# Turning the normalised rows of eight of sixteen query chunks by DMA instead of TensorE

## The reference

```
kv = x @ W.T;  K, V = split(kv);  a = softmax(x @ K.T + causal) @ V
x1 = layernorm(x + (x + a))
xr, xk = mu * x1 + (1 - mu) * x1 of the token before
y  = layernorm(x1 + x1 + sigmoid(xr @ W_r.T) * (relu(xk @ W_k.T)**2 @ W_v.T))
```

## Time and profile before

| | us |
|---|---|
| three runs | 1156.16, 1182.71, 1183.41 |
| median of them | 1182.71 |
| the profiled execution, its own time | 1158.02 |
| its slowest core (core 5), first to last instruction | 1156.5 |
| its other cores | 1151.0 to 1155.3 |
| outside the span: 1158.02 less 1156.5 | 1.5 |

### The profile page before, as it was taken

How to read it: one execution, slowest core, us unless ns; L and a number is a source line. 1 busy time by engine, 2 the same in 40 slices (tenths; PEclk the granted TensorE clock), 3 DMA queues, 4 the chain that set the end, 5 groups by cost and what they waited for, 6 DMA issues and landing times.

```text
span 1156.5 us, 18353 instructions; the slowest of 8 cores (1151.0 to 1156.5 us)
## 1 busy us (share of the span) xinstructions
PE 1142.9 (99%) x6138; PEld 599.4 (52%) x6138; DVE 609.2 (53%) x907; ACT 448.1 (39%) x737; POOL 275.7 (24%) x354
## 2 busy tenths in 40 slices
PE   8999999999999999999999999999999999999996
PEld 3444444444444455454454557888874444444442
DVE  3545555633343142454432457876666675576865
ACT  4443333432232021223211334666564443336664
POOL 0000000000000011122111234533223333279882
PEclk9999999999999999999999999999999999999999
DMA  7455366653153152456546665776436654566662
GB/s 190 138 178 166 108 200 200 200 173 101 49 160 119 28 95 75 119 170 163 146 116 169 174 187 147 226 213 198 144 122 188 192 167 135 174 227 231 224 219 91
DMA packets 141932, 182.77 MB, mean 158 GB/s; under 512 B 44048, under 2 KB 95504, under 8 KB 141840
## 3 DMA queue, kind: packets, MB, share of 16 engines
q1 hardware_dynamic: 134512, 155.92, 45.0%
q0 software_dynamic: 7328, 25.69, 7.6%
HBM read 108.18 MB, written 64.49 MB: 149 GB/s over the span
## 4 chain that ended last, share of the span: by engine, by line
PE 98%; DVE 1%; DMA 1%; issue 0%; ACT 0%; DVEq 0%; POOLq 0%; ACTq 0%
PE ps L736 27%; PE ps L737 27%; PE ps L738 27%; PE ps L905 3%; PE ps L904 3%; PE ps L903 3%; PE ps L906 3%; PE ps L907 3%; PE ps L902 3%; PE ps L825 1%; DMA STG<-x 1%; PE ps L750 0%; PE ps L755 0%; PE ps L754 0%; DVE X L1194 0%
## 5 line engine op out<-in xcount | busy, mean ns | idle before, releaser
L669 POOL TENSOR_TENSOR SU<-TP 128x256 f32<-128x256 f32 x48 | 42.4, 883 | 184.3 <-DVE TP L1084 136.0
L1143 DVE TENSOR_TENSOR OUT<-SN,ps 128x512 f32<-128x512 f32 x94 | 63.9, 680 | 35.6 <-PE ps L738 34.6
L637 POOL DMA_DIRECT2D Z<-xtok x16 | 8.8, 553 | 289.2 <-PE ps L738 288.3
L1143 DVE TENSOR_TENSOR SN<-SN,ps 128x512 f32<-128x512 f32 x72 | 49.2, 683 | 37.9 <-PE ps L738 37.0
L706 POOL DMA_DIRECT2D x1t<-XTS x32 | 24.4, 764 | 173.2 <-ACT XTS L1349 173.2
L1333 ACT ACTIVATE PROB<-ps,NEGM 128x512 f32<-128x512 f32 (+3 forms) x36 | 22.6, 633 | 104.0 <-DVE NEGM L1036 104.0
L1349 ACT COPY XTS<-ps 128x512 f32<-128x512 f32 x32 | 18.4, 585 | 112.6 <-PE ps L825 112.6
L1068 DVE SCALAR_TENSOR_TENSOR Z<-ps,RZ,Z 128x512 f32<-128x512 f32 x16 | 12.0, 749 | 73.8 <-PE ps L907 72.9
L1455 ACT ACTIVATE OUT<-OUT 128x512 f32<-128x512 f32 x32 | 20.1, 627 | 65.0 <-DVE OUT L1143 64.9
L684 POOL TENSOR_TENSOR X<-X,RR 128x512 f32<-128x512 f32 x30 | 40.8, 1372 | 11.2 <-DVE RR L1185 11.1
L670 POOL TENSOR_TENSOR SU<-TP 128x256 f32<-128x256 f32 x48 | 41.4, 862 | 6.9
(11 more groups left out here) (449 smaller groups left out, 3504.6 us busy)
## 6 DMA issues: line engine op xcount, KB each, us to landing
STG<-x1t SPq DMA_DIRECT2D x64, 256.5 KB, 4.2
STG<-x SPq DMA_DIRECT2D x56, 256.0 KB, 4.8
WA<-wc SPq DMA_DIRECT2D x28, 512.0 KB, 6.0
Z<-xtok POOLq DMA_DIRECT2D x16, 512.0 KB, 4.5
x<-Z POOLq DMA_DIRECT2D x16, 512.0 KB, 4.2
x1t<-XTS POOLq DMA_DIRECT2D x32, 256.0 KB, 2.8
ka<-OUT SPq DMA_DIRECT2D x32, 256.0 KB, 3.4
r<-OUT SPq DMA_DIRECT2D x32, 256.0 KB, 2.6
```

The costliest lines, as they stand in the source:

```text
L669: step(gp.tensor_tensor(s1, a21, a22, op=ALU.add))
L1143: ve.tensor_tensor(out, a, ps, op=ALU.add).then_inc(count, 1)
```

## The change

Chunks at `POS` 0 to 7 (15, 3, 14, 2, 13, 1, 0, 12; `BY_DMA = 8`) are no longer transposed by TensorE. A float32 is seen as two 16-bit words. POOL copies the high words and then the low words of each half row of `Z` into a buffer `ZP[i]`, two copies of 128 x 512 words for each half, four per chunk. SP turns each `ZP[i]` with one DMA transpose into `ZT[i]`. ACT puts the words together again in `XTS[i]`, two copies with a step of two words for each half. POOL stores `XTS` as before.

The steps are spread over turns: POOL's copies of a chunk come in the turn after its own, SP's transposes (`turn_rows`) stand in the second turn after its own, behind that turn's probabilities, ACT's copies stand in the third, ahead of the exponentials, and POOL's store of chunk m - 2 stands behind its copies of chunk m. The other eight chunks keep the way through TensorE, and all of their `flip_x` stand at the end of a turn. The loads of `XQ[1]` (`xq1a`, `xq1b`), their casts, and the loads of weight slots 6 and 4 move one turn on. The new buffers take 8 KB per partition; for them the memory that POOL's DMAs keep for descriptors is cut from 16,384 to 8,192 bytes per partition.

```diff
-BASE = 16_416
+SCRATCH = 8192
+BASE = SCRATCH + 32
-    nc = bass.Bass("TRN2", target_bir_lowering=False)
+    nc = bass.Bass("TRN2", target_bir_lowering=False, dynamic_dma_scratch_size=SCRATCH)
+    ZP = [at(f"ZP{i}", [128, 1024], U16, oY + i * 2 * KB) for i in range(2)]
+    ZT = [at(f"ZT{i}", [128, 1024], U16, oY + 4 * KB + i * 2 * KB) for i in range(2)]
-    CASTS = {12: N["xq1a"], 11: N["xq1b"]}
+    CASTS = {11: N["xq1a"], 10: N["xq1b"]}
@@ SP
+        def turn_rows(q):
+            for i in range(2):
+                sy.wait_ge(g_zp, t_x(q, i) + 1)
+                if POS[q] > 0:
+                    sy.wait_ge(a_xt, t_x(q, i) - 1)
+                sy.dma_start_transpose(out=ZT[i].rearrange("p (c s) -> p c s", s=128), in_=ZP[i]).then_inc(ld_zt[i], 16)
         for q in ORDER:
             for g in range(G(q)):
                 turn(q, g)
+            if 2 <= POS[q] < BY_DMA + 2:
+                turn_rows(ORDER[POS[q] - 2])
-            elif q == 0:
+            elif q == 12:
                 loads(N["xq1a"][0], N["xq1b"][0] + 1)
-            elif q == 12:
+            elif q == 11:
                 stored(sy.wait_ge, range(12))
...
@@ POOL
+        def store_x1t(m):
+            q = ORDER[m]
+            for i in range(2):
+                gp.wait_ge(a_xt, 2 * m + i + 1)
+                dst = x1t_d[i * 512:(i + 1) * 512, (q + 1) * 128:(q + 2) * 128].rearrange("(c p) s -> p c s", p=128)
+                gp.dma_start(out=dst, in_=XTS[i].rearrange("p (c s) -> p c s", s=128)).then_inc(st_xt[i], 16)
             gp.dma_start(out=x1_d[q * 128:(q + 1) * 128, :], in_=Z[m % 2]).then_inc(st_x1[m % 2], 16)
-            for i in range(2):
-                gp.wait_ge(a_xt, 2 * m + i + 1)
...
+            if m < BY_DMA:
+                for i in range(2):
+                    if m > 0:
+                        gp.wait_ge(ld_zt[i], 16 * m)
+                    words = Z[m % 2][:, i * 512:(i + 1) * 512].bitcast(U16).rearrange("p (s w) -> p w s", w=2)
+                    gp.tensor_copy(ZP[i][:, 0:512], words[:, 1, :])
+                    gp.tensor_copy(ZP[i][:, 512:1024], words[:, 0, :]).then_inc(g_zp, 1)
+                if m > 1:
+                    store_x1t(m - 2)
+            else:
+                if m == BY_DMA:
+                    store_x1t(m - 2)
+                    store_x1t(m - 1)
+                store_x1t(m)
             if m < 14:
                 gp.wait_ge(st_x1[m % 2], 16 * (m // 2 + 1))
+                if m < BY_DMA:
+                    gp.wait_ge(g_zp, 2 * m + 2)
                 load_z(ORDER[m + 2])
@@ TensorE
-            elif q in (0, 12):
-                scores(SCORES[q][0:1])
-                flip_x(13 if q == 0 else 1, 0)
-                flip_x(13 if q == 0 else 1, 1)
-                scores(SCORES[q][1:])
...
-                if g == n - 1 and q < 15 and n > 1:
+                if g == n - 1 and POS[q] > BY_DMA:
                     flip_x(prev, 0)
@@ ACT
         def rows_t(q, i):
+            if POS[q] > 0:
                 sc.wait_ge(st_xt[i], 16 * POS[q])
+            if POS[q] < BY_DMA:
+                sc.wait_ge(ld_zt[i], 16 * (POS[q] + 1))
+                words = XTS[i].bitcast(U16).rearrange("p (s w) -> p w s", w=2)
+                sc.copy(words[:, 1, :], ZT[i][:, 0:512])
+                sc.copy(words[:, 0, :], ZT[i][:, 512:1024]).then_inc(a_xt, 1)
+            else:
+                sc.wait_ge(pe_t, t_x(q, i) - 2 * BY_DMA + 1)
+                sc.copy(XTS[i], PS[4 + i]).then_inc(a_xt, 1)
-            softmax(SCORES[q], after(q))
+            softmax(SCORES[q], after(q), ORDER[POS[q] - 3] if 3 <= POS[q] < BY_DMA + 2 else None)
```

More of the change, by code:

```diff
@@ L9 @@
 BF16 = mybir.dt.bfloat16
+U16 = mybir.dt.uint16
 AF = mybir.ActivationFunctionType
@@ L161, in build_program @@
     ld_pt = [sem(f"ld_pt{i}") for i in range(5)]
+    ld_zt = [sem(f"ld_zt{i}") for i in range(2)]
     st_o = [sem(f"st_o{i}") for i in range(3)]
@@ L338, in t_x @@
         return 2 * POS[q] + i
-    def t_bank(q, i):
-        return PS[5] if q == 15 else PS[4 + i]
+    BY_DMA = 8
     def stage(n):
@@ L702, in gpsimd_program @@
             gp.dma_start(out=x1_d[q * 128:(q + 1) * 128, :], in_=Z[m % 2]).then_inc(st_x1[m % 2], 16)
-            for i in range(2):
-                gp.wait_ge(a_xt, 2 * m + i + 1)
-                dst = x1t_d[i * 512:(i + 1) * 512, (q + 1) * 128:(q + 2) * 128].rearrange("(c p) s -> p c s", p=128)
-                gp.dma_start(out=dst, in_=XTS[i].rearrange("p (c s) -> p c s", s=128)).then_inc(st_xt[i], 16)
+            if m < BY_DMA:
[12 more added lines that the diff above has]
+                store_x1t(m)
             if m < 14:
                 gp.wait_ge(st_x1[m % 2], 16 * (m // 2 + 1))
+                if m < BY_DMA:
+                    gp.wait_ge(g_zp, 2 * m + 2)
                 load_z(ORDER[m + 2])
@@ L810, in flip_x @@
         def flip_x(q, i):
-            e = t_x(q, i)
             te.wait_ge(v_x1, POS[q] + 1)
-            if e == 0:
-                te.wait_ge(v_p, 64)
-            elif e == 1:
-                te.wait_ge(a_xt, 1)
-            elif q == 3 and i == 0:
-                te.wait_ge(a_exp, first(2) + 1)
-            elif q == 14:
+            if POS[q] == BY_DMA:
                 te.wait_ge(a_exp, first(1 - i) + 1)
             else:
-                te.wait_ge(a_xt, e - 1)
+                te.wait_ge(a_xt, t_x(q, i) - 1)
             for j in range(4):
                 c = i * 512 + j * 128
-                mm = te.transpose(t_bank(q, i)[:, j * 128:(j + 1) * 128], Z[POS[q] % 2][:, c:c + 128], IDN)
+                mm = te.transpose(PS[4 + i][:, j * 128:(j + 1) * 128], Z[POS[q] % 2][:, c:c + 128], IDN)
             mm.then_inc(pe_t, 1)
@@ L873, in tensor_program @@
                 product(0, 2, (0, 1, 2))
-            elif q == 3:
-                scores(SCORES[q][0:2])
-                flip_x(15, 0)
-                scores(SCORES[q][2:])
-            elif q == 13:
-                for i in range(2):
-                    scores(SCORES[q][i:i + 1])
-                    flip_x(14, i)
-            elif q in (0, 12):
-                scores(SCORES[q][0:1])
-                flip_x(13 if q == 0 else 1, 0)
-                flip_x(13 if q == 0 else 1, 1)
-                scores(SCORES[q][1:])
             else:
@@ L909, in tensor_program @@
                         mm.then_inc(pe_pv, 1)
-                    if g == n - 1 and j == 0 and (n > 1 or q == 3) and q < 15:
+                    if g == n - 1 and j == 0 and POS[q] > BY_DMA:
                         flip_x(prev, 1)
@@ L1345, in rows_t @@
         def rows_t(q, i):
-            sc.wait_ge(pe_t, t_x(q, i) + 1)
-            if q < 15:
+            if POS[q] > 0:
                 sc.wait_ge(st_xt[i], 16 * POS[q])
-            sc.copy(XTS[i], t_bank(q, i)).then_inc(a_xt, 1)
+            if POS[q] < BY_DMA:
[6 more added lines that the diff above has]
+                sc.copy(XTS[i], PS[4 + i]).then_inc(a_xt, 1)
         def scale(x):
@@ L1391, in high_probs, with softmax @@
                 high_p_t(q, g)
-        def softmax(blocks, nxt):
+        def softmax(blocks, nxt, turned_rows=None):
             chunks = ended(blocks)
@@ L1397, in softmax @@
                 high_probs(nxt, 0, 2)
+            if turned_rows is not None:
+                rows_t(turned_rows, 0)
+                rows_t(turned_rows, 1)
             for c in chunks:
@@ L1409, in scalar_program @@
                 high_sums(MIXES[prev])
-            if q == 3:
-                rows_t(15, 0)
-            elif q in (13, 0, 12):
-                for i in range(2):
-                    rows_t({13: 14, 0: 13, 12: 1}[q], i)
-            softmax(SCORES[q], after(q))
+            softmax(SCORES[q], after(q), ORDER[POS[q] - 3] if 3 <= POS[q] < BY_DMA + 2 else None)
             if q == 13:
@@ L1420, in scalar_program @@
                 scale(MIXES[q])
-            if G(q) > 1 and q < 15:
-                rows_t(prev, 0)
-                rows_t(prev, 1)
-            elif q == 3:
-                rows_t(15, 1)
-            if q == 12:
+            if q == 11:
                 sc.wait_ge(pe_s, first(12) + 4)
@@ L1431, in scalar_program @@
                 high_probs(after(q), at_once(after(q)), 2)
+            if POS[q] == BY_DMA + 1:
+                rows_t(ORDER[BY_DMA - 1], 0)
+                rows_t(ORDER[BY_DMA - 1], 1)
+            if POS[q] > BY_DMA:
+                rows_t(prev, 0)
+                rows_t(prev, 1)
             if q in MIXES:
```

10 lines of the change are left out of this document (4 added, 6 removed).

## The result

The changed kernel took 1177.68 us in the median of its 6 runs (1176.01 to 1293.32), the kernel before 1157.47 in the median of 6 (1156.16 to 1183.41). The ratio is 1.018, 95% interval 1.0162 to 1.0197: within 2%, but a loss of some 20 us where I had forecast a gain of 7.

The account below looks back on a forecast made before the run. TensorE was taken to bound the kernel, busy 1142.9 of 1156.5 us. From 1158.0, 64 transposes at 0.11 (7.0) were removed and no waits added, giving 1151 us; range 1147 to 1178.

Parts of the forecast that it names:

- the account itself: Whole kernel: TensorE work removed less TensorE waits added, from the profiled 1158.0 us, 7.0 less, giving 1151.0.
- something else: Any outcome outside the forecast case and the named rivals, no place or size given; chance 0.02.
- The range's top: Upper end of the predicted time, set at 1178 us from the earlier runs' 1183.41 less 7.0, which is 1176.4.
- Transposes at 0.11 each: Attention turns 1 to 8: 64 transposes leave TensorE at 0.11 us each from start to start, 7.0 us in all.
- Rival D: Each transpose removed from TensorE is worth its whole 0.273 us, 17.5 in all, time 1140.5; chance 0.03.
- The walk and the hiding: Short turns before chunk 12: its first block's transpose issued at 510.4, landing 513.8, wanted 518.1, so no TensorE wait.
- c: Time of one POOL copy of 128 x 512 16-bit words: 0.9 us taken, bounds 0.55 and 2.26.
- B: Short turns: the POOL, store, ACT, SP loop closes too slowly; TensorE waits 10.2 us, time 1161 to 1171; chance 0.1.
- A: At chunk 12, row transposes land late and TensorE waits 1.3 to 6.4 us, time 1152 to 1157.5; chance 0.2.
- The second tight place: Chunk 11's first scores wait on chunk 12's first exponential: slack 0.15 us before and after, added wait taken as 0.
- Rival C: At attention's end, a load or weight slot timed by DMA comes last and eats the gain, 1156 to 1160; chance 0.1.

Follow-up runs that it names:

- `before_again`: The kernel before, unchanged, run again: 1156.72 us at the lower level, ratio 0.9999; 1 of 9 runs at the upper level.
- `mem_only`: The kernel before with only the changed kernel's memory layout (descriptor memory 8192 bytes, buffers lower): 1156.61 us at the lower level, ratio 0.9996.
- `twice_third`: The changed kernel with each of its 64 remaining TensorE transposes issued twice, a later rerun: 1157.13 us at the lower level, ratio 1.0000.
- `no_flip`: The kernel before without TensorE's row transposes of the eight first chunks, rows left untransposed (wrong results): 1148.60 us at the lower level, ratio 0.9929.
- `twice`: The changed kernel with each of its 64 remaining TensorE transposes issued twice: 1157.70 us, ratio 0.9989, when first run; 1157.41 and 1157.13 in reruns.
- `after_fourth`: The changed kernel, unchanged, run once more: 1149.97 us at the lower level, ratio 0.9937; 3 of 6 runs at the upper level.
- `rows_early`: The changed kernel with ACT's row copies put back ahead of the casts in turns 9 to 15: 1151.91 us, ratio 0.9937; reruns 1149.04 and 1149.05.
- `no_warm`: The changed kernel with 1 instead of 10 warm-up products before the first projection: 1152.99 us, ratio 0.9953; reruns 1151.07 and 1151.02.
- `tail_pad`: `rows_early` with 64 tiny products added at the end of TensorE's list: 1150.61 us, ratio 0.9938, beside its control's 1149.05.

## Why the prediction was wrong, and where it was right

**The step that failed** is the account itself: "PE work removed less PE waits added, made against the profiled execution". It takes for granted that stages which the change doesn't touch keep their time, and it counted the 27 us between the kernel before's own runs as noise of the measurement ("three runs of one program differ by 27 us"). They are two levels of one mechanism: a granted clock of 0.81 for 161 us in the projections, on pairs of cores. The slowest core makes the time, so one pair is enough. What decides is how often it comes. Over the chips that show it at all (A, B, E), the runs of the programs with the full count of TensorE instructions (before, `before_again`, `mem_only`, `twice_third`) had it in 11 of 71 cases, those with 64 fewer and 10 warm-up products (the changed kernel, `no_flip`) in 14 of 21. By comparison it is 2 of 6 against 5 of 5 in the first, 6 of 38 against 6 of 10 on B, and 3 of 27 against 3 of 6 on E. (For the first comparison's runs of before only the times are known; two are at 1183.) So the first comparison had it in all of the changed kernel's runs and in 2 of 6 of before's, and a median turned that into plus 20 us. (The ratio of 1.018 sets runs of the changed kernel at the upper level against the four of the kernel before at the lower one, 1156 to 1158.) None of the named rivals was this; it fell under "something else", at 0.02. The range's top, 1178, was set by exactly this ("the runs of one program reach 1183.41; less 7.0 this is 1176.4") and held the time, with luck, by 0.3 us; I had priced the level rightly and its frequency not at all.

**Transposes at 0.11 each**: right. 171.81 became 164.82, and `twice` beside the changed kernel gave the 7 back (1157.41 against 1150.18, 1157.13 against 1149.97). Rival D, 0.273 each, would have been 17.5. `no_flip`, the ceiling, ends where the changed kernel ends at the lower level on chip B (two runs each).

**The walk and the hiding**: right, with errors that cancelled. One of POOL's copies takes 0.61 us, and the four in a row start 0.55 apart (496.36, then the stores at 498.58), which is the lower bound of c and not the 0.9 that I used: 1.4 us less for four. The stores' landing and ACT's copies (0.76 each and not 0.6) took 1.0 more than forecast, and SP needed 3.07 for its two issues, so that chunk 12's block came 0.75 later behind ACT than worked out. The sum is the 0.3 between 510.4 and 510.7. The row transposes landed after 3.8 in the median, 6.6 at most. B did not occur. A occurred once that I found, on core 2 of `after_fourth`: PE waits for a block of chunk 12; the four transposes of probabilities around it landed after 4.5 to 11.5 us:

```profile
524.74 0.38 PE L916 MATMUL ps<-V2H,PT 128*128 128x512 bf16 x1 [0.71 <-DMA PT<-PH]
```

It was not that core's loss that set the time. The descriptor memory cost nothing (`mem_only`).

**The second tight place**, chunk 11's first scores with 0.15 of slack: right. They start at 497.37, 0.39 behind the matmul before them, and before it was 0.38.

**Rival C**, the gain goes elsewhere, happened in part, 0 to 2.3 us per core, but not by a load or weight slot: by ACT's list, an edit that I described in one clause and did not price. It was the moved `rows_t`, past a cast that waits for a DMA.

**A gain I did not see**: some 1 us at the start. At the lower level the changed kernel gained 6.9 us on D and E, and `rows_early`, which is rid of the waits just named, 8.0 on D and F. That is 1 more than the transposes' 7.0, and it fits the start. In the two profiles of D no core of these kernels begins its products later than 7.8 us, and one core of each pair of the kernel before begins at 7.7 to 8.5, and most of those run some us at half pace (profiles of A and B). So a gain of 6.9 is luck in part: 1 gained at the start and 1 lost at the end of attention, neither in the forecast. The 7.0 of turns 1 to 8 is no luck.

**What stays open.** Why the length of TensorE's program changes when the first weights are usable, I can't say; no row shows it. That close starts bring on the low clock is supported, not shown: in the profiles of A, B and E with 10 warm-up products, among pairs whose waits for the first weights differ by 1.05 us or less, 4 of 15 were caught, and of those that differ by 1.2 or more, none of 17. The ends of the cores, which follow the starts but for 0 to 2.3 us of later waits, are on record for more runs: of pairs that end within 1.0 us of each other 21 of 86 were caught, of those 1.1 to 2.4 apart 4 of 74, and of those 2.5 or more apart 2 of 184. Closeness isn't all of it: within 1.0 us it is 7 of 44 in the programs with the full count and 14 of 42 in the others. `no_warm` never had it on chip E (0 of 4), too few to tell. That the frequency follows LENGTH rests on counts over few chips, and `tail_pad`, which would have tested it best, ran on a chip without the effect.

## What to carry to other kernels

When a kernel's own runs fall into two levels, find the mechanism before predicting (here one look at the clock of each core), and treat its frequency as something that an edit can move, however far from it in time. Compare cores that are not touched by it as well as the median: those gave the change's worth within about 1 us when the median said plus 20. And when a wait-free copy is moved behind an instruction that waits for a DMA, price that edit like any other: here it cost about 1 us (1150.18 against 1149.04 on chip D, with overlapping intervals).

## What the runs showed of the hardware

- A granted clock of 0.81 for 160 to 161 us from 12 us on, on both cores of a pair at once, one or two pairs at a time, on chips A, B and E; it ended at 173 with PE busy as before. On chip C the same level came for 4 to 5 us at a time on one die. The Trainium skill, TensorE: Matmul & The Clock Gate, Part 1, says of a limiter at 13/16 that it takes the whole die once a third core starts dense matmuls and holds while the load lasts. The level agrees (616 of 749 matmuls is 0.82). The extent and the release of the 160 us form do not: 165 of 221 executions, all with eight cores at work, have a mean clock of 0.99 or more on every core, and where this form comes it takes pairs and lets go under load.
- 64 tiny products more at the very end of TensorE's list made the first weights late on one core of each pair: waits of 1.66 to 2.88 us, where no core of the control waits over 1.20 (one profile of each). Why is open.
- After a wait of 2.55 us before the first products, core 1 of `before_again` ran at a granted clock of 0.51 for 3.4 us. After one of 2.21, core 5 of `before` ran at half pace until 14.4 (starts 0.43 us apart instead of 0.215), while the granted clock reads 1.00.
- Copies of 128 x 512 16-bit words with a step of two, on core 5 of the changed kernel: 0.61 us on POOL (1.07 at most), 0.55 from start to start, and 0.76 on ACT. DMA transposes of 128 x 1024 such words beside POOL's loads and stores: 3.0 to 6.6 us to landing there, up to 8.2 on the other cores.
